# Edge tiles at the border of two node blocks, summed once into 128 nodes that span the border (two-stage GNN kernel, one core)

## What is computed

```python
# stage 1: x1 = layernorm(x + L0(x)), with neighbour sums of weighted rows
messages = edge_val[:, None] * embeddings[edge_src]
neighbor_emb = segment_sum(messages, edge_dst, num_segments=3125)
# stage 2: x2 = layernorm(x1 + L1(x1))
e   = relu(ea @ ee_w1 + ee_b1) @ ee_w2 + ee_b2
msg = x[src] + e                         # x is stage 1's result
agg = segment_sum(msg, dst, num_segments=n)
h = (1.0 + eps) * x + agg                # 256 columns
h = relu(_ln(h @ w1 + b1, g1, be1))      # 256 -> 1024
h = relu(_ln(h @ w2 + b2, g2, be2))      # 1024 -> 1024
y = h @ w3 + b3                          # 1024 -> 256
out = relu(_ln(x + y, bn_g, bn_b))
```

## Time and profile before

| | us |
|---|---|
| median of 3 executions | 1523.69 |
| lowest and highest of them | 1514.35, 1540.35 |
| the profiled execution: its time | 1535.62 |
| its span in the trace | 1533.7 |
| stage 2 in that span (from about 735 us to the end) | about 800 |
| busy in the span: PE | 1254.0 (82%) |
| busy in the span: DVE | 959.9 (63%) |
| busy in the span: POOL | 824.7 (54%) |
| busy in the span: ACT | 678.4 (44%) |
| mean clock granted to TensorE, as a share of 2.4 GHz | 0.874 |

### The profile page before, as it was taken

The page is one execution under the profiler, slowest core; times in us unless marked ns, Lnnn a source line. Parts: engine busy times, 40 slices in busy tenths (PEclk is TensorE's granted clock), DMA queues, the critical chain, the costliest instruction groups (busy, mean ns, idle before and its releaser), DMA issues.

```text
span 1533.7 us, 21066 instructions
## 1 busy us (share of the span) xinstructions
PE 1254.0 (82%) x5295; PEld 993.8 (65%) x5295; DVE 959.9 (63%) x2787; ACT 678.4 (44%) x1654; POOL 824.7 (54%) x840
## 2 busy tenths in 40 slices
PE   4888878888879978877877878886888788878997
PEld 3666666666667666766655756665667667656776
DVE  4766666776666776766744655554565556546665
ACT  2455555565555664545332423332443334323443
POOL 6656555666556666654654564443555456544530
PEclk9788889998878989889988988888898889979999
DMA  6435445555455444546654564544555556554530
GB/s 194 114 112 154 140 134 154 159 155 157 141 146 145 133 134 129 157 126 184 186 153 127 154 189 129 148 141 121 158 154 160 153 145 178 156 149 136 161 111 16
DMA packets 106088, 222.13 MB, mean 145 GB/s; under 512 B 20003, under 2 KB 57369, under 8 KB 106010
## 3 DMA queue, kind: packets, MB, share of 16 engines
q0 software_dynamic: 53408, 164.16, 38.3%
q1 hardware_dynamic: 52602, 57.11, 12.1%
HBM read 203.96 MB, written 17.23 MB: 144 GB/s over the span
## 4 chain that ended last, share of the span: by engine, by line
PE 49%; another core or an unknown queue 15%; issue 14%; DVE 10%; ACT 10%; DMA 1%; POOL 0%; DVEq 0%; ACTq 0%; POOLq 0%; SPq 0%
PE ps_z L1307 21%; PE ps_e L1040 8%; PE ps_y L1307 4%; PE ps_sum L1045 4%; PE ps_sum L1047 4%; PE ps_s L1262 3%; ACT msg L1579 3%; DVE msg L2071 2%; DVE msg L2077 2%; ACT msg L1582 2%; ACT aF L1804 2%; PE ps_tr L1376 2%; DVE oh L159 1%; PE ps_w L1141 1%
## 5 line engine op out<-in xcount | busy, mean ns | idle before, releaser
L963 POOL DMA_INDIRECT grow<-table_dram,src_all x401 | 386.0, 963 | 379.5 <-PE ps_s L1262 250.1
L908 POOL DMA_INDIRECT raw<-in_x,src_all x399 | 404.5, 1014 | 257.4 <-DVE msg L2077 143.7
L1307 PE MATMUL ps_z<-w_high,a 128*128 128x512 f32 x784 | 292.3, 441 | 77.3 <-issue 60.5
L2071 DVE SCALAR_TENSOR_TENSOR msg<-raw,w_sb,msg 128x256 fp32r<-128x256 f32 x416 | 183.8, 482 | 212.2 <-ACT msg L1582 139.0
L1040 PE MATMUL ps_e<-we,attr 65*128 65x256 f32 x832 | 254.9, 431 | 47.2 <-DVE msg L2077 36.6
L1045 PE MATMUL ps_sum<-msg,oh 128*128 128x512 f32 x464 | 251.9, 543 | 29.7 <-DVE msg L2077 23.0
L1307 PEld LDWEIGHTS ps_z<-w_high,a 128*128 128x128 f32 x784 | 167.1, 214 | 130.6 <-issue 78.6
L1582 ACT ACTIVATE msg<-ps_e 128x512 fp32r<-128x512 f32 (+1 forms) x220 | 124.1, 564 | 254.3 <-remote 158.9
L1040 PEld LDWEIGHTS ps_e<-we,attr 65*128 65x128 f32 x832 | 175.2, 217 | 94.7 <-issue 62.0
L159 DVE TENSOR_SCALAR oh<-lane,rel 128x128 fp32r<-128x128 f32 x915 | 209.4, 291 | 3.6 <-issue 3.4
L1047 PE MATMUL ps_sum<-msg,oh 128*128 128x512 f32 x464 | 203.0, 437 | 6.3 <-issue 6.2
(11 more groups left out here) (182 smaller groups left out, 1577.8 us busy)
## 6 DMA issues: line engine op xcount, KB each, us to landing
attr<-in_attrT SPq DMA_DIRECT2D x50, 192.0 KB
raw<-in_x,src_all POOLq DMA_INDIRECT x416
grow<-table_dram,src_all POOLq DMA_INDIRECT x401
w_raw<-in_m_w SPq DMA_DIRECT2D x48, 128.0 KB
table_dram<-table SPq DMA_DIRECT2D x23, 256.0 KB
attr<-in_attrT SPq DMA_DIRECT2D x24, 160.0 KB
xs<-in_x SPq DMA_DIRECT2D x24, 128.0 KB
xTb<-in_xT SPq DMA_DIRECT2D x24, 128.0 KB
```

Of the source, the lines that this page charges most:

```text
L908: pool.indirect_dma_start(out=raw[:, j, :], out_offset=None, in_=x, in_offset=bass.IndirectOffsetOnAxis(ap=src_all[:, q * TILES + j:q * TI ...
L963: pool.indirect_dma_start(out=grow[:, j, :].bitcast(F32), out_offset=None, in_=table_dram, in_offset=bass.IndirectOffsetOnAxis(ap=src_all[ ...
L1307: mm = pe.matmul(acc, left[a], right[b], start=False, stop=stop and a == 1, skip_group_check=True)
L2071: dve.scalar_tensor_tensor(msg[:, j, 1, 0:D], raw[:, j, :], w_sb[:, tile_cols(n, j)], msg[:, j, 0, 0:D].bitcast(F32), ALU.mult, ALU.subtract)
```

## The change

Between the 128 nodes of one block and those of the next lies a window of 128 nodes: the last 64 of the one and the first 64 of the other. Tile 16 of a block and tile 0 of the next touch only nodes of that window. From position 2 on (`WINDOWS`) they are summed once, into the window, in columns 256 to 511 of `ps_y`:

- PE: `tile_kind` says for each tile of a step whether it is summed as before (LANES), into the window (WINDOW), or not at all. For p > 2 step c = 0 and tile 0 of step c = 1 fall away. Steps 8 and 9 (p >= 2) go into the window, by two products of 128x256 for a tile, one for the high and one for the low part, both onto the same 256 columns (`add_window_tile`). The first of them waits for `window_open`.
- ACT: `open_window` writes zeros to these columns, after `carried`.
- DVE: one one-hot for each tile that is summed, 17 in place of 19 for a position; those of the window compare with lanes that are shifted by 64 (`make_window_lanes`, three copies, once). `take_h` has a third addition, 64 partitions by 256 columns, that adds the window's upper half to the block's last 64 nodes; it waits for `y_done` of layer 3 of the same round. `carry`, after `h_low`, adds the window's other half to the first 64 rows of the next block's `hbx`; it waits for that load.
- POOL: tile 16 of a position now waits for step c = 8 of the position before (`row_free`), no longer for step c = 0 of its own.
- The test of the targets at the start (`bad`) has three parts in place of two, for each of the two borders tried. On the inputs here the stricter test holds for a border of one tile, so that the same path is taken.

The diff, cut to its core:

```diff
+    def tile_kind(self, p, c, j):
+        span = self.steps[c][0]
+        if behind_window(p) and (c == 0 or span == 0 and j < self.edge):
+            return None
+        if has_window(p) and (span == 1 or span == 0 and j >= TILES - self.edge):
+            return WINDOW
+        return LANES
...
     def row_free(self, p, k):
...
-        if PAIRS[k][0] + PAIRS[k][1] <= TILES - self.edge:
+        if has_window(p - 1) or PAIRS[k][0] + PAIRS[k][1] <= TILES - self.edge:
             return 0 if p == 1 and k >= LAST_PAIRS else SUMS * (p - 1) + k + 1
         return SUMS if p == 1 else SUMS * p + 1
...
+                def add_window_tile(j, slot):
+                    for half in range(2):
+                        mm = pe.matmul(ps_y[:, D:2 * D], oh[:, slot, :], grow[:, j, half * D:(half + 1) * D],
+                                       start=False, stop=False, skip_group_check=True)
+                    return mm
...
                 def near_step(path, p, c):
...
                     for j in range(j0, j0 + m):
+                        kind = path.tile_kind(p, c, j)
+                        if kind is None:
+                            continue
+                        if kind == WINDOW and (c, j) == path.first_window(p):
+                            pe.wait_ge(window_open, p - WINDOWS + 1)
                         pe.wait_ge(got[j], 16 * path.fills(p + span, j))
...
+                def open_window(p):
+                    wait(act, carried, p - WINDOWS)
+                    act.activation(ps_y[:, D:2 * D], lane[:, 0:D], ACT.Copy, scale=0.0).then_inc(window_open, 1)
...
                     if exists(i - 2):
                         finish_std(i - 2, 1)
+                    if exists(i + 1):
+                        open_window(i + 1)
...
-                dve.tensor_scalar(bad[:, n, :, 0:edge], rel[:, :, 0:edge], float(-P), None, ALU.is_lt)
-                dve.tensor_scalar(bad[:, n, :, edge:TILES], rel[:, :, edge:TILES], 0.0, None, ALU.is_lt)\
-                   .then_inc(prep, 1)
+                parts = ((slice(0, edge), -HALF, HALF), (slice(edge, lim), 0, P), (slice(lim, TILES), HALF, P + HALF))
+                for part, low, _ in parts:
+                    ins = dve.tensor_scalar(bad[:, n, :, part], rel[:, :, part], float(low), None, ALU.is_lt)
+                ins.then_inc(prep, 1)
...
                     dve.wait_ge(h_half, loaded)
-                    dve.tensor_tensor(h[:, :], ps_s[:, D:2 * D], h[:, :], ALU.add).then_inc(h_ready, 1)
+                    if not (windows and has_window(b)):
+                        dve.tensor_tensor(h[:, :], ps_s[:, D:2 * D], h[:, :], ALU.add).then_inc(h_ready, 1)
+                        return
+                    dve.tensor_tensor(h[:, :], ps_s[:, D:2 * D], h[:, :], ALU.add).then_inc(h_summed, 1)
+                    dve.wait_ge(h_summed, b - WINDOWS + 1)
+                    dve.wait_ge(y_done, b - 1)
+                    dve.tensor_tensor(h[HALF:P, :], ps_y[HALF:P, D:2 * D], h[HALF:P, :], ALU.add)\
+                       .then_inc(h_ready, 1)
+
+                def carry(b):
+                    dve.wait_ge(hb_in, 16 * (b + 1))
+                    dve.tensor_tensor(hbx[0:HALF, :], ps_y[0:HALF, D:2 * D], hbx[0:HALF, :], ALU.add)\
+                       .then_inc(carried, 1)
...
                     if exists(i):
                         h_low(i)
+                    if exists(i + 1):
+                        carry(i)
```

89 lines of the change are left out of this document (70 added, 19 removed).

## The result

The changed kernel is slower: 1704.47 us (median of 5, 1692.0 to 1715.15) against 1532.55 us for the kernel before beside it (median of 5, 1514.35 to 1541.73). The ratio is 1.1185, with a 95% interval of 1.1059 to 1.1311. I had forecast 1528.

What follows compares the result with a forecast made beforehand. Most rounds were taken as paced by POOL's gathers holding the engines, despite PE 82% busy. Halted rounds +5.4, free rounds -1.6, start +0.5 sum to +4.3 us; from the median 1523.69 that gives 1528, range 1500 to 1548.

Steps and rivals of the forecast that it cites:

- PE's term: PE, positions 3 to 24: two 128x512 products fewer, window products slightly dearer; -0.41 us each, -9.0 if PE sets the pace.
- The additions: New operations on DVE and ACT: third addition of take_h (0.42 us), carry, open_window (0.371 us); all expected hidden behind other waits.
- The half microsecond for the stricter test: At the start, four more small operations for the targets' test: 0.8 us at most, taken as 0.5.
- the hole of 1.96 us: POOL's stop between its fifth and sixth gather of a round, assumed to remain, with the second run ending 0.46 us later.
- the upper end: Case where an event of PE ends POOL's hole: second run ends 0.84 us later, +0.8 us a halted round.
- +0.3 was summed for 18 rounds: Halted rounds, paced by POOL's gathers: +0.3 us each, between +0.0 and +0.8; 18 rounds give +5.4 us.
- the 1522 to 1540: Main case, rounds paced by the gathers as worked out, +0.0 to +0.8 us a round; chance 0.45.
- The circle: Most rounds: PE's first sum releases gathers, gathers hold the engines, their release lets PE reach the next first sum.
- the fetch of instructions: Guess at what halted engines lack during POOL's gathers: their instructions, which also come by DMA; no size given.
- The halts change in kind: Rival: loops' code moves, halts of 6.7 us fall away in a fifth or more of rounds; 34 us, 1490; chance 0.08.
- Four rounds are free: Rounds without a halt, at PE's pace: four at -0.41 us each, -1.6 us in the sum.
- The slower rival: Second gather run starts unmoved with 13 gathers: +22 to +30 us; 1540 to 1554, chance 0.11; beyond 1554, 0.06.

Runs made afterwards that it cites:

- two gaps: Changed kernel, tiles 4 and 5 released by the round's last sum step, POOL also waiting ahead of tiles 8 and 12: 1442.28 us; on another chip 1470.64.

## Why the prediction was wrong, by its own steps

**PE's term held.** I took -0.41 us a position and -9.0 in all; with the gathers out it is 22.86 - 22.40 = 0.46, and 9.9. The counts (365 and 92, three ahead of layer 1) are as said.

**The additions were hidden as said.** open_window and carry waited 0.0 us, the third addition of take_h 7.3 us in 23, nearly all of it for layer 3's increment, y_done; with two gaps, where that is less late, it waits 0.8 us. The half microsecond for the stricter test can't be seen: take_h of the first full round came at 790.70, before at 791.96.

**The failed step** is this: "With one gather less ahead of it and the same hole the second run starts at t + 8.27, and it has thirteen." I took the hole of 1.96 us for something fixed, or else (the upper end) for an event of PE that moves with PE. The earlier trace rows named the releaser, PE's ps_s, and I did not ask which product that was and when it had ended. The third step ended at 1107.98, POOL could ask for it from 1110.0, and it went on at 1111.66: a wait for a product that had been over for two microseconds is itself the sign that something is held. With the gathers 0.46 us later in the round and the transposes 0.48 us earlier, the first landings fell behind the transposes' increments and not ahead of them, and the hole did not move but vanished: 17 gathers in one run and 7.7 us a round more, where +0.3 was summed for 18 rounds. Where a hole, of 2.6 us, was put back by force, the time came out at 1535.51 us, within the 1522 to 1540 that the sum gave.

**The circle was right in shape and wrong in its link.** "The gathers hold the engines" stood there, and that halts end 2.2 to 2.8 us behind the run of gathers; it is 3.2 in the round shown. But the link was a guess, the fetch of instructions, and with it a halt could only shift by the time by which the run shifts. The link that the runs bear out, held increments that come out in a stop, makes the time of a round depend on whether there is a stop. The instruction queues would have told me: in the 200 us from 1000 on they carry this, in the changed kernel and in the one before.

```profile
q14 instruction: 2, 0.02, 0.0%
```

```profile
q14 instruction: 1, 0.01, 0.0%
```

Five or six rounds with one or two instruction packets are not halted by fetches. The Trainium skill's rule on taken branches (Runtime: NRT & Kernel Launch, Instruction fetch mechanics), which I had put beside my guess, has no part in these halts.

**The rival was there with the wrong sign.** "The halts change in kind" had 0.08, priced as halts falling away: "Nothing in the rows asks for it." The rows had both signs in them. Among the rounds of before there are some of 23 to 25 us, and others of 43 to 47; in these POOL has no hole of 2 us behind the fifth gather, only stops of 0.5 to 1.4 us, as in the run from 1350.21 on (0.76, 0.67 and 0.67). A kernel that falls into either kind from round to round is near a threshold, and a shift of 0.9 us decided for nearly all rounds. The price did not stand there ready: each of these long rounds is followed by one of 23 to 25 us (44.0 by 22.9), so that a pair costs 2 to 9 us more than two of 31.6, while in the changed kernel the long rounds follow each other. So the sum's "Four rounds are free" does not hold either: these rounds come behind the long ones. The slower rival (thirteen gathers, 1.25 us later, +22 to +30) was right in sign, but its mechanism is not what happened.

**The range** of 1500 to 1548 went by the spread of before's executions and by the two ends of the hole. Neither end was "no hole".

## What to carry to other kernels

Where an engine waits for TensorE, look at when the product it waits for had ended; if that is microseconds earlier, the wait is not for the product, and here its price did not add up from durations. A round's time that comes in two or three kinds (24, 31, 45 us) was the sign of such a threshold here: price a change at each kind, not only at the mean. Gathers by a list on GpSimd that run beside work which other engines take from TensorE can be worth breaking up; three stops of 2 to 3 us among 17 gathers took the kernel before, which looked bound by TensorE, to 0.963 of its time (0.9545 to 0.9715), and the changed kernel to 0.9537 of that time (0.9407 to 0.9667).

## What the runs showed of the hardware that I had not expected

- While POOL issues gathers by a list and they land, the semaphore increments of TensorE are late, up to 18 us (1169.51 to 1187.43). They come out in order, singly and mostly 1.4 to 2.9 us apart at first, and the rest together (42 ns apart from 1110.90 to 1111.15), 1.2 and 3.2 us behind POOL's last issue in the two rounds shown; those of ScalarE and VectorE are on time (within 0.01 us). Stage 1, whose rows POOL gathers by a list too, shows the same: in the kernel before 252 of the 490 increments of TensorE on record up to 735 us come more than 1 us late.
- Plain loads of the same bytes do nothing of the kind, from SP's queue or from POOL's own (1307.54 to 1338.26 us against 1701.06 and 1711.49 for lists of rows).
- The stops' length and number both matter, and they were not varied one by one: 0.6 us was too short (1633.79), one of 2.6 took the loss back (1535.51), one or two more of 2.0 to 2.4 gained (1442.28 to 1485.22), and one of 3.8 in place of 2.4 gave 1517.5, on another chip than the 1485.22.
- A load of 128 rows costs POOL 544 ns as a plain one and 950 by a list.
- Without the gathers from the third block on, the kernel before takes 1334.8 us, 199 below the 1533.82 beside it: the bound by TensorE that the page suggests lies that much lower than where the kernel stands.
